# A row of maxima for latent attention: two DMAs from SBUF to SBUF in place of a store to memory and a load

## The reference

```
q = (x @ Wq).reshape(b, t, H, D).transpose(0, 2, 1, 3)
ckv = x @ Wkva
kv_latent, k_rope = (ckv[:, :, :R], ckv[:, :, R:])
kv = (kv_latent @ Wkvb).reshape(b, t, H, NOPE).transpose(0, 2, 1, 3)
...
att = jnp.einsum('bhqd,bhkd->bhqk', q, k) / jnp.sqrt(jnp.float32(D))
att = jnp.where(mask, att, jnp.float32(-jnp.inf))
att = jax.nn.softmax(att, axis=-1)
y = jnp.einsum('bhqk,bhkd->bhqd', att, v)
```

## Time and profile before

| | |
|---|---|
| median of three runs | 2611.51 us (2609.6 to 2611.68) |
| profiled execution | 2615.5 us, span 2613.7 us, granted clock 0.965 in the mean |
| busy over the span | TensorE matmuls 91%, weight loads 75%, VectorE 69%, ScalarE 52%, GpSimd 35% |
| DMA packets of ScalarE's queue (q10) | 1792, 0.53 MB |
| latent attention, first to last score | 437.3 to 1500 us |

### The profile page before, as it was taken

One profiled execution on the slowest core, in us unless ns is written; L12 is line 12 of the kernel. 1 busy time (PEld: TensorE's weight loads), 2 busy tenths in 40 slices (PEclk: granted clock), 3 DMA queues, 4 the chain that ended last, 5 costly groups with the idle time before them and its releaser, 6 DMA issues. The chain is left out here.

```text
span 2613.7 us, 45553 instructions
## 1 busy us (share of the span) xinstructions
PE 2391.2 (91%) x16852; PEld 1972.2 (75%) x16852; DVE 1814.0 (69%) x3344; ACT 1348.6 (52%) x2031; POOL 927.5 (35%) x1046
## 2 busy tenths in 40 slices
PE   6999868999999999999999969999678888999998
PEld 4777655777777777777777768888567776888887
DVE  6888874886778767876787656666566657666664
ACT  5666543766666666666666733332234433333322
POOL 1233333464546454645444321221346641010000
PEclk9999988999999999999999979999889998999999
DMA  4011104433343334333433252332301103221222
GB/s 142 27 35 52 30 30 133 124 107 106 100 143 107 96 110 142 107 105 90 139 106 108 63 181 68 97 100 74 129 9 35 35 31 129 42 76 40 77 58 41
DMA packets 193805, 223.83 MB, mean 86 GB/s; under 512 B 37400, under 2 KB 157232, under 8 KB 189936
## 3 DMA queue, kind: packets, MB, share of 16 engines
q1 hardware_dynamic: 191792, 220.38, 29.0%
q10 hardware_dynamic: 1792, 0.53, 0.1%
HBM read 150.95 MB, written 55.73 MB: 79 GB/s over the span
## 5 line engine op out<-in xcount | busy, mean ns | idle before, releaser
L1240 DVE TENSOR_REDUCE l_negmax<-l_mx 128x1 f32<-128x512 f32 (+3 forms) x608 | 391.7, 653 | 90.9 <-PE l_mx L1639 88.5
L1253 DVE TENSOR_TENSOR l_Plo<-l_s,l_Phi 128x512 fp32r<-128x512 f32 x576 | 368.6, 681 | 22.9 <-ACT l_s L1492 21.6
L1488 ACT ACTIVATE l_Phi<-l_s 128x1024 fp32r<-128x1024 f32 x288 | 295.1, 1025 | 170.8 <-PE l_s L1661 162.2
L1672 PE MATMUL l_o<-l_Phi,l_V 128*128 128x256 f32 x1152 | 308.6, 290 | 14.1 <-ACT l_Osb L1500 10.7
L1672 PE MATMUL l_o<-l_Plo,l_V 128*128 128x256 f32 x1152 | 299.7, 282 | 0.0
L1492 ACT ACTIVATE l_s<-l_s 128x1024 f32<-128x1024 f32 x288 | 295.0, 1024 | 0.0
L2788 ACT ACTIVATE m_hidhi<-m_h 128x512 fp32r<-128x512 f32 x168 | 106.2, 632 | 358.5 <-DVE m_h L2637 356.3
L1659 PE MATMUL l_s<-l_QA,l_KK 128*128 128x512 f32 x576 | 270.6, 470 | 10.5 <-DMA l_QB<-l_md 6.0
L1639 PE MATMUL l_mx<-l_KK,l_QA 128*128 128x512 f32 (+3 forms) x768 | 271.3, 393 | 8.3 <-DVE l_negmax L1240 2.9
L1672 PEld LDWEIGHTS l_o<-l_Phi,l_V 128*128 128x128 f32 x1152 | 218.9, 190 | 57.0 <-issue 28.5
L1661 PE MATMUL l_s<-l_QB,l_KL 65*128 65x512 f32 x576 | 228.5, 397 | 0.0
(11 more groups left out here) (469 smaller groups left out, 6396.6 us busy)
## 6 DMA issues: line engine op xcount, KB each, us to landing
l_qd<-l_qs SPq DMA_DIRECT2D x256, 128.0 KB, 2.4
l_QA<-l_qd SPq DMA_DIRECT2D x64, 512.0 KB, 3.6
l_QB<-l_qd SPq DMA_DIRECT2D x64, 256.0 KB, 4.4
l_R<-l_rd SPq DMA_DIRECT2D x128, 128.0 KB, 2.9
m_spread<-m_combs SPq DMA_DIRECT2D x62, 256.0 KB, 5.1
m_spread<-m_combs SPq DMA_DIRECT2D x124, 128.0 KB, 5.1
xs<-next_store SPq DMA_DIRECT2D x32, 256.0 KB, 2.0
l_rps<-l_rp SPq DMA_DIRECT2D x128, 64.0 KB, 1.9
```

Source lines behind the costliest of these rows:

```text
L1240: v.tensor_reduce(negmax[:, n % 2, at + h0:at + h1], piece_of(number, chunk), AX.X, ALU.max, negate=True).then_inc(reduced, 1)
L1253: v.tensor_tensor(Plo[:, s % 3, x].rearrange("p h q -> p (h q)"), S2[s % 2][:, x * HALF:(x + 1) * HALF], Phi[:, s % 3, x].rearrange("p h q ...
L1488: a.activation(Phi[:, s % 3].rearrange("p u h q -> p (u h q)"), S2[s % 2][:, :], ACT.Exp, scale=L_D ** -0.5).then_inc(exped, 1)
L1672: mm = pe.matmul(O[:, odd * 2 * P:(odd + 1) * 2 * P].rearrange("p (j q) -> p j q", j=2), V[:, b % 2, k, 64 - 64 * odd:192 - 64 * odd], src ...
```

## The change

The copy into mrow stays. From mrow two DMAs go straight to partition 64 of QB, one for each query tile, with four partitions each as source; both are issued at unit 4, one after the other. The tensor MD, the semaphore `mstored` and `max_down` are gone. The wait for the old content of QB (`scored`) moves from `max_down` to `max_row`, and `mready` counts 32 a step instead of 16.

```diff
             def max_row(n):
                 a.wait_ge(filled, L.use["max", n] + 1)
                 if n >= 2:
-                    a.wait_ge(mstored[n % 2], 16 * (n // 2))
+                    a.wait_ge(mready[n % 2], 32 * (n // 2))
                 a.activation(mrow[:, n % 2, :], PJ[0:8, 0:P], ACT.Copy).then_inc(freed_a, 1)
-                if n >= 2:
-                    a.wait_ge(mready[n % 2], 16 * (n // 2))
                 a.wait_ge(freed_a, L.after("max", n))
-                a.dma_start(MD[n % 2], mrow[:, n % 2, :].bitcast(F32)).then_inc(mstored[n % 2], 16)
-
-            def max_down(n):
-                a.wait_ge(mstored[n % 2], 16 * (n // 2 + 1))
                 if n >= 4:
                     a.wait_ge(scored, UNITS * (n - 3))
-                a.dma_start(QB[64:65, n % 4].bitcast(F32),
-                            MD[n % 2:n % 2 + 1].rearrange("o (t h) q -> o h t q", t=2)).then_inc(mready[n % 2], 16)
+                for t in range(2):
+                    a.dma_start(QB[64:65, n % 4, :, t, :].bitcast(F32),
+                                mrow[4 * t:4 * t + 4, n % 2, :].bitcast(F32)).then_inc(mready[n % 2], 16)
...
                 if i == 4 and L.is_step(m + 1):
                     max_row(m + 1)
-                if i == 6 and L.is_step(m + 1):
-                    max_down(m + 1)
...
                 if u % UNITS == 0:
-                    pe.wait_ge(mready[m % 2], 16 * (m // 2 + 1))
+                    pe.wait_ge(mready[m % 2], 32 * (m // 2 + 1))
```

More of the change, by code:

```diff
@@ L1000, in latent_attention @@
         QD = dram("qd", (2, 4, 32, 4, 2 * P))
-        MD = dram("md", (2, 8, P))
         SD, RD = dram("sd", (2, 2, 2, 2 * P)), dram("rd", (2, 2, 4 * P))
@@ L1021, in latent_attention @@
         wlow = signal("wlow")
-        qswap, qstored, mstored, mready = ([signal(f"{n}{i}") for i in range(2)]
-                                           for n in ("qswap", "qstored", "mstored", "mready"))
+        qswap, qstored, mready = ([signal(f"{n}{i}") for i in range(2)] for n in ("qswap", "qstored", "mready"))
         sstored, sready, rstored, rready = ([signal(f"{n}{i}") for i in range(2)]
```

## The result

The changed kernel takes **2629.89 us**, the median of four runs (2627.92 to 2632.12), against 2611.6 us of four runs of the kernel before beside it. The ratio is 1.0061, 95% interval 1.0045 to 1.0076: 18.3 us slower, where +9.0 was forecast, and beyond the end of the range at 2626. Its profiled execution took 2627.92 us, span 2626.1, mean granted clock 0.964.

The account below looks back on a forecast made before the run. TensorE's hand-written order was taken as the bound, its waits adding directly: 31.9 us added, less 14.7 of row waits and 8.2 hidden, gave +9.0, so 2620.5 us; 8-in-10 range 2601 to 2626.

Parts of the forecast that it names:

- Cheap: Rival: each new DMA issue on ScalarE costs 0.27 us like the store; net -10.8, 2600.7 us; chance 0.20.
- medium: Rival: issues of 0.47 us each, or more slack than found; net about -1, 2610.5 us; chance 0.21.
- The row's waits: TensorE's weight loads waiting at step boundaries for the row of maxima through memory: all 14.7 us go.
- the row still ends last: Rival: DMA landing of 3.3 us makes the row 0.5 late in eight steps; +4 on top, 2624.5 us; chance 0.04.
- Items 1 to 3: Output-bank evacuations delayed behind the issues, n mod 16 = 6, 8; 5, 9; 10, 12: 7.7, 7.6 and 5.6 us added.
- item 2: n mod 16 = 5, 9: exponential, evacuation, exponential back to back, so the evacuation inherits the delay; 7.6 us added.
- Item 4: n = 3, 17, 33, 49: delayed exponential delays VectorE's low part and TensorE's load, without slack; 3.6 us added.
- Item 5: n mod 16 = 2, 4: first score newly waits for VectorE's low part, 0.54 us in eight steps; 4.3 us added.
- What hides part of it: Later VectorE-set waits in the same step absorb delay: 2.0 us, 4.2 before next batch's transposes, 2.0 at n = 12; 8.2 together.
- item 6: n mod 16 = 0, 14 and n = 61: 3.1 us added in eight steps, with one gain in step 29.
- Item 7: All other steps: nothing added, since TensorE has an output projection there and the low part is ready early.
- nothing hides: Rival: 0.63 us per issue and no absorption of 6.2 us in batches one to three; +17.8, 2629.3 us; chance 0.06.

Follow-up runs that it names:

- the removal: Narrow 32-column group replaced by two matmuls of 256 columns in batches 1 to 3, in both kernels: kernel before 2604.23 us, changed 2616.39 us.
- hold_long: Against the kernel with both DMAs at unit 6: two unread ScalarE copies, with semaphore waits, added behind the row's copy, no DMA at unit 4; 2623.37 us.

## Why the prediction was wrong, step by step

The sign and the mechanism came out; the size was half. To place the difference, each of the some 6100 weight loads of the stage in the changed kernel was set beside its counterpart before, and the growth of the lag at each was put down to what the load waits for.

- *What bounds it*: right. TensorE's busy time in the stage is 1024.7 against 1019.2 us, with no matmul more, and 1022.3 in a second profile of the kernel before; the difference is waits and clock.
- *The issues*: 0.60 taken, 0.58 measured; ScalarE's next instruction 0.93 us later where 0.97 was said. "Cheap" and "medium" issues are out. The Trainium skill, "DMA: Bandwidth & Descriptors", section "Issuing engines are not separate DMA queues", calls this time usually small beside the DMA itself (the 50 ns that the prediction quotes stand there in a section on the path of GpSimd, not on ScalarE's); here two issues that nothing covers hold the queue for 1.2 us, and their place in the order moves the kernel by 27 us.
- *The row's waits*: all 14.7 us gone, as said; so is the rival in which the row still ends last.
- *Items 1 to 3*, the evacuations: 7.7, 6.4 and 5.3 us against 7.7, 7.6 and 5.6. Right, item 2 a little high.
- *Item 4*: 3.5 against 3.6 us. Step 16 in the changed kernel, which answers to the earlier trace rows (0.20 us of waiting before, 1.09 now):

```profile
719.41 1.03 ACT L1481 ACTIVATE l_Phi<-l_s 128x1024 fp32r<-128x1024 f32 x1 [1.36 <-PE l_s L1652]
...
721.38 1.29 DVE L1251 TENSOR_TENSOR l_Plo<-l_s,l_Phi 128x512 fp32r<-128x512 f32 x2 [1.19 <-ACT l_s L1485]
...
722.13 0.10 PEld L1648 LDWEIGHTS l_s<-l_maskT,identb 128*128 128x128 bf16 x1 [1.09 <-DVE l_Plo L1251]
```

- *Item 5*: in step 33 it is 4.09 us from the first issue to the first score of step 34, against 5.15; 1.06 us won, 1.16 said. The new wait, 0.54 us, is the one that was predicted; the view writes "issue" beside it, but the load starts 0.12 us behind the end of the first of VectorE's two low parts, at 1014.71:

```profile
1010.74 1.20 ACTq L1474 DMA_DIRECT2D l_QB<-l_mrow  x2
...
1014.02 1.29 DVE L1251 TENSOR_TENSOR l_Plo<-l_s,l_Phi 128x512 fp32r<-128x512 f32 x2 [0.81 <-ACT l_s L1485]
...
1014.83 0.10 PEld L1648 LDWEIGHTS l_s<-l_maskT,identb 128*128 128x128 bf16 x1 [0.54 <-issue]
```

- ***"What hides part of it", 8.2 us: this step failed*** in two of its three parts. The 2.0 us at n = 5, 21, 37, 53 are right. Of the 4.2 us ahead of the next batch's transposes only 1.5 were hidden (1.3 to 2.0 over three profiles). In step 8 the evacuation came 0.86 us later at the weigh, and the wait of 1.67 us shrank only by 0.52, since VectorE's rows came later as well:

```profile
577.55 0.59 ACT L1493 ACTIVATE l_Osb<-l_o 128x512 f32<-128x512 f32 x1
...
579.94 0.42 PEld L1553 LDWEIGHTS l_pj<-ident,next_rows 128*128 128x128 f32 x4 [1.15 <-issue]
```

VectorE's rows slip by the 0.3 us that I had said, but beyond a delay that they already carry. Counted from the first score, TensorE is 1.95 us later than before when this evacuation comes, the 0.99 us of n = 8 in it, and so are the rows that VectorE normalizes by then; the rows that the transposes wait for are 2.28 later. So nothing of the delay of n = 8 could be hidden, and of that of n = 9 only 0.86 less 0.33 us, the 0.52 measured, and not 1.67 less 0.3. And the 2.0 us behind n = 12 were no slack at all. The 0.81 us at 632.06 carry VectorE's name, but in the changed kernel the score there is behind the same gap, to the digit, with no one to wait for:

```profile
645.69 1.93 PE L1559 MATMUL l_pj<-l_rT,l_wkva 128*64 128x512 f32 x4
```

```profile
646.60 0.14 PEld L1559 LDWEIGHTS l_pj<-l_rT,l_wkva 128*64 128x64 f32 x1 [0.29 <-issue]
647.55 0.19 PEld L1650 LDWEIGHTS l_s<-l_QA,l_KK 128*128 128x128 f32 x1 [0.81 <-issue]
```

The gap behind this group of 512-column matmuls is 0.81 us in all 120 places in all 20 traces, whoever is named. By that I read it as time that the matmul ahead keeps the next weight load out; no run tried it by itself. In all 3.5 us were hidden, not 8.2. Other terms took part of that back: the evacuations were 1.5 us less, item 6 came to some 1.3 us instead of 3.1, and a wait that the sum did not name, for the queries' load in step 3, shrank from 1.54 us to 0.17. Item 7, put at nothing, was 1.5 to 1.9 us at n mod 16 = 15. What is left outside the half-speed stretches is +10.6, +10.1 and +11.3 us in the stage in the three profiles, against 9.0. So the 9.0 was near the waits' part by errors that partly cancel.

- ***A term that the sum did not have: TensorE's clock.*** The loads in and right behind the half-speed stretches carry +7.7, +5.2 and +6.4 us in the same three profiles, and the 64 columns take 7.1 us off the difference of the two kernels, the removal 6.1. The rows said 1.00 for the stage, and I took that as a property of the stage rather than of how its work lies in time. Its only 3.4 us at half speed, at 1193.7 us right behind the third of the narrow groups, was in the trace and was not looked for. With 64 columns in both kernels, so like for like and with the clock kept, the difference is 11.2 us, where 9.0 was forecast.
- The rival *nothing hides* gave 2629.3 us and is right by its number alone: it had 17.8 us of waits, and there are some 11.

What stays open: why moving ScalarE's work by a microsecond lets the clock fall behind all three groups instead of one or two. The groups themselves have the same matmuls in both kernels. The kernels with evacuation waits of 19 us and more had 16 of 18 groups followed by half speed, the others 11 of 27; this goes together, but no run separates how the waits ahead would act on it.

## What to carry to other kernels

Count a DMA issue on a compute engine as time of that engine (0.27 to 0.63 us here, by the form of the transfer), and place it behind an instruction that keeps its datapath busy, never between a small copy and the instruction for which the bottleneck engine waits; one longer issue was cheaper than two. A wait may be taken as cover only if it changes from step to step: a gap that is the same to the hundredth wherever the same matmul stands ahead is most likely that matmul's. And before summing waits, list the stretches at half clock and what work they follow, for here a shift in time multiplied them. Where narrow matmuls finish no sooner than wider ones, as here with 32 and 64 columns, the wider ones are worth a trial.

## What the runs showed of the hardware

- The issue of a DMA into one partition of SBUF from another tile took 0.581 us in the median with four partitions as source and 0.627 with eight; the store of the same eight partitions to memory took 0.27, and of two or four of them 0.28 and 0.26. The cost of an issue went by the form, hardly by the bytes.
- An activation started 0.09 us before the end of the one ahead of it. Behind a semaphore wait for that one's end it started 0.03 us after the end (526.38 against 526.35 in hold_long).
- TensorE's clock fell to the 1.2 GHz level in the middle of work that is recorded as busy without a gap, around the end of 32 matmuls of 32 columns in 27 of 45 cases, and in none of 9 with 64 columns, at the same 273 ns for one and 3.7 us for the group. The Trainium skill, "TensorE: Matmul & The Clock Gate", section "What's actually happening", ties the clock to how busy the engine has been recently. The busy time of the profile, 6.80 of 6.80 us ahead of the fall, does not bear this out here.
